# Forgetting attention's inverse roots: from ScalarE's Ln and Exp per four units to a Newton chain on GpSimd per two units

## The reference, cut to what matters

```python
q = x @ Wq; k = x @ Wk; v = x @ Wv
k = short_conv(k, kconv_w); v = short_conv(v, vconv_w)      # 4 taps, then silu
q = group_rmsnorm(q, qnw, H); k = group_rmsnorm(k, knw, H)  # x / sqrt(mean(x^2 per head) + 1e-6) * w
cum = jnp.cumsum(jax.nn.log_sigmoid(x @ Wf + bf), axis=1)
scores = q k^T / 8 + cum_t - cum_s, causal; attn = softmax(scores)
out = attn @ v
rms = jnp.sqrt(jnp.mean(jnp.square(out), axis=-1, keepdims=True) + EPS)
out = out / rms * onw * (g * jax.nn.sigmoid(g))             # g = x @ Wg
return out.reshape(Bx, Tx, H * Dh) @ Wo
```

## Time and profile before

| | |
|---|---|
| median of 3 runs | 2406.13 us (2402.49 to 2408.33) |
| profiled execution | 2402.83 us, of which 2401.0 us span |
| busy shares of the span | PE 80%, DVE 66%, ACT 59%, POOL 37% |
| the block that is changed | about 911 to 1960 us of the span |
| last unit begins its scores | 1914 us |

### The profile page before, as it was taken

The page is one execution under the profiler, slowest core; times in us unless marked ns, Lnnn a source line. Parts: engine busy times, 40 slices in busy tenths (PEclk is TensorE's granted clock), DMA queues, the critical chain, the costliest instruction groups (busy, mean ns, idle before and its releaser), DMA issues. The chain is left out here.

```text
span 2401.0 us, 35531 instructions
## 1 busy us (share of the span) xinstructions
PE 1915.7 (80%) x11731; PEld 871.1 (36%) x11731; DVE 1592.8 (66%) x2337; ACT 1406.1 (59%) x2262; POOL 890.3 (37%) x722
## 2 busy tenths in 40 slices
PE   4457886377775765799999999999999966599997
PEld 2113331343453422344444444444444422222222
DVE  4979995686347756678888888888887535511212
ACT  2446662333333434577777777777776533699994
POOL 0156663244014421345555455555555422500001
PEclk9769997598896987899999999999999988899998
DMA  2000000000000001111111111111112100412110
GB/s 90 0 14 0 0 0 0 1 1 1 0 1 0 1 7 47 47 49 58 57 57 58 57 58 57 57 58 58 57 58 64 45 23 11 121 40 54 47 47 36
DMA packets 66146, 86.15 MB, mean 36 GB/s; under 512 B 13344, under 2 KB 37216, under 8 KB 65888
## 3 DMA queue, kind: packets, MB, share of 16 engines
q1 hardware_dynamic: 60944, 81.37, 11.0%
q10 hardware_dynamic: 5040, 2.72, 0.4%
HBM read 72.12 MB, written 11.93 MB: 35 GB/s over the span
## 5 line engine op out<-in xcount | busy, mean ns | idle before, releaser
L1634 DVE SCALAR_TENSOR_TENSOR fu_kv<-fu_ps_kv,fa_vec,fu_kv 128x511 f32<-128x511 f32 x366 | 252.7, 738 | 7.1 <-ACT fu_kv L1542 6.3
L1991 ACT ACTIVATE rt_p<-rt_ps_s 128x1024 f32<-128x1024 f32 x256 | 240.4, 1042 | 26.2 <-PE rt_ps_o L1936 17.4
L1706 POOL TENSOR_TENSOR fu_p<-fu_p 128x768 f32<-128x768 f32 x64 | 116.7, 1824 | 262.2 <-PE fu_ps_n L1392 257.8
L1362 PE MATMUL fu_ps_s<-fu_qn,fu_kn 64*128 64x512 f32 (+3 forms) x1024 | 190.1, 469 | 7.5 <-ACT fu_p L1529 5.6
L601 POOL TENSOR_TENSOR scan_hC<-scan_h,scan_c 128x1024 f32<-128x1024 f32 x64 | 150.7, 2354 | 82.4 <-DVE scan_h L581 82.4
L1392 PE MATMUL fu_ps_n<-fu_p,fu_vt 128*64 128x512 f32 (+3 forms) x1024 | 166.3, 446 | 0.0
L526 PE MATMUL scan_ps_y<-scan_hC,w_ident 128*128 128x512 f32 x256 | 129.6, 630 | 41.5 <-POOL scan_hC L601 24.8
L581 DVE TENSOR_TENSOR_SCAN scan_h<-scan_dA,scan_ps_b 128x1024 f32<-128x1024 f32 x64 | 146.4, 2287 | 2.2
L1936 PE MATMUL rt_ps_o<-rt_p,rt_va 128*32 128x512 f32 x1024 | 138.1, 611 | 10.0 <-ACT rt_p L1991 8.1
L1717 POOL TENSOR_TENSOR fu_num<-fu_num,fu_sg 128x512 f32<-128x512 f32 x64 | 81.2, 1269 | 172.1 <-DVE fu_sg L1667 172.1
L1420 PE MATMUL fu_ps_kv<-w_XN,fa_wp 128*128 128x512 f32 x244 | 125.3, 637 | 17.6 <-DVE fu_cr L1599 15.3
(11 more groups left out here) (346 smaller groups left out, 4903.4 us busy)
## 6 DMA issues: line engine op xcount, KB each, us to landing
fu_rb<-rms_rows SPq DMA_DIRECT2D x256, 128.0 KB, 2.9
fu_ro<-rms_rows SPq DMA_DIRECT2D x128, 128.0 KB, 2.9
ra_stackq<-rope_parts SPq DMA_DIRECT2D x168, 32.0 KB
ra_stackk<-rope_parts SPq DMA_DIRECT2D x168, 32.0 KB
rms_rows<-fu_r SPq DMA_DIRECT2D x14, 192.0 KB, 2.1
w_X<-in_xT SPq DMA_DIRECT2D x4, 512.0 KB
fa_wp<-in_wp SPq DMA_DIRECT2D x8, 256.0 KB
fu_cr<-ncum_rows SPq DMA_DIRECT2D x128, 3.0 KB
```

The source lines that it names most:

```text
L1362: pe.matmul(sps[:, h, at:at + T - t * P], k[head(h), t * P:(t + 1) * P], q[head(h), t * P:T], start=(at == 0), stop=False)
L1634: dve.scalar_tensor_tensor(acc, projected(a, k)[:, 0:T - j], vec[:, a % GA, at:at + 1], acc, ALU.mult, ALU.add).then_inc(done, 1)
L1706: pool.tensor_tensor(tail, tail, P13[:, :, 0:3 * P], ALU.add).then_inc(s.d1, 1)
L1991: act.activation(pr[k % 2][i][:, :, :], sps[(U * n + u) % RING][:, :, :], ACT.Exp, scale=DH_B ** -0.5).then_inc(s.exp, 1)
```

## The change

WIN becomes 2, so a window slot is every second one (`i % 2 == 1`), and 32 windows take the place of 16. AHEAD stays 8 (now 4 WIN), OUT goes from 5 to 4 (WIN + 2), and with it the `wo` products move from odd to even slots.

ACT no longer does Ln, Exp and the preload. It gets the query and key sums instead (Identity with the epsilon as bias, `msq`), placed ahead of the four squares. DVE keeps the addition for outputs. SP folds the sums by SBUF-to-SBUF DMAs from MS ([rows, 512]) into VAR ([96, 64]), so that 32 partitions hold what were 4 rows. DVE makes a first guess of the inverse root from the bits (shift and xor, [96, 64]). POOL refines it: five operations in the window slot, six in the next, each waiting for the one before. SP stores the roots a slot later, and reads them for RB and RO from there on. On DVE, OG moves from the head of the slot to behind the taps, ahead of the bit operation and of reduce L1650. ACT's and DVE's special orders for window slots go.

```diff
-WIN = 4
+WIN = 2
+ROOT_SCALE = 1.8348544414191587e-20
-    AHEAD = 2 * WIN
-    OUT = WIN + 1
+    AHEAD = 4 * WIN
+    OUT = WIN + 2
+    ROWS = 2 * WIN
+    FOLD = 32 // ROWS
+    CUT = T // FOLD
-        q, o = i // WIN + 1, i // WIN - 1
+        q, o = i // WIN + 3, i // WIN - 1
+    def folded(j):
+        return 32 * (min(j, U // WIN) + max(j - 4, 0))
+        VAR, ROOT, STEP1, STEP2 = (st.sb(n, [96, CUT]) for n in ("var", "root", "step1", "step2"))
...
 # SP
-                    if i % WIN == 1 and windows(i - 1) != (None, None):
-                        j, r = (i - 1) // WIN + 1, rows_of(*windows(i - 1))
+                    if i % WIN == 1 and windows(i - 3) != (None, None):
+                        j, r = (i - 3) // WIN + 3, rows_of(*windows(i - 3))
                         sp.wait_ge(s.r, j + 1)
                         sp.wait_ge(s.put, 16 * j)
                         sp.dma_start(rows_dram[j, r, :], R[j % 2][r, :]).then_inc(s.put, 16)
-                    u = i - OUT
+                    u = i - OUT - 1
...
+                    if i % WIN == 1 and windows(i - 1) != (None, None):
+                        j, r = (i - 1) // WIN + 3, rows_of(*windows(i - 1))
+                        sp.wait_ge(s.r, j)
+                        sp.wait_ge(s.msq, min(j + 1, U // WIN))
+                        sp.wait_ge(s.mso, max(j - 3, 0))
+                        for g in range(3):
+                            if g < 2 and r.start == 0:
+                                sp.dma_start(VAR[32 * g:32 * g + 32, :], MS[32 * g:32 * g + ROWS, :]).then_inc(s.fold, 16)
+                            elif g == 2 and r.stop == 96:
+                                for h in range(2):
+                                    sp.dma_start(VAR[64 + 16 * h:80 + 16 * h, :], MS[64 + ROWS * h:64 + ROWS * h + WIN, :]).then_inc(s.fold, 16)
 # ACT
+                    if q is not None:
+                        act.wait_ge(s.sa, WIN * q + WIN)
+                        act.wait_ge(s.fold, folded(q))
+                        act.activation(MS[0:64, :], ssps[0:64, :], ACT.Identity, bias=w.eps_rms[0:64, 0:1]).then_inc(s.msq, 1)
...
-                        act.preload_act_table_set("natural_log_exp_and_others")
...
-                        act.activation(MS[r, :], MS[r, :], ACT.Ln).then_inc(s.ln, 1)
...
-                        act.activation(R[j % 2][r, :], MS[r, :], ACT.Exp, scale=-0.5).then_inc(s.r, 1)
 # DVE
-                    (OG at the head of the slot)
-                    if q is not None:
-                        dve.tensor_scalar(MS[0:64, :], ssps[0:64, :], RMS_EPS, None, ALU.add).then_inc(s.msq, 1)
+                    (behind the taps, ahead of reduce L1650)
+                    if real(o):
+                        dve.wait_ge(s.gated, o + 1)
+                        dve.wait_ge(s.ro, 32 * (o + 1))
+                        dve.wait_ge(s.wo, o // 2)
+                        dve.scalar_tensor_tensor(OG[o % 2][:, :], NUM[o % NR][:, :], ow[:, o % GA:o % GA + 1], RO[:, :], ALU.mult, ALU.mult).then_inc(s.og, 1)
+                    if q is not None or v is not None:
+                        j, r = (i - 1) // WIN + 3, slice(0, rows_of(q, v).stop)
+                        dve.wait_ge(s.fold, folded(j + 1))
+                        dve.wait_ge(s.r, j)
+                        dve.tensor_scalar(ROOT[r, :].bitcast(I32), VAR[r, :].bitcast(I32), 1, 0x7fffffff, ALU.logical_shift_right, ALU.bitwise_xor).then_inc(s.bits, 1)
 # POOL, behind its three additions; x, y, e, f = VAR, ROOT, STEP1, STEP2
+                    (window slot; each waits for the one before)
+                        pool.wait_ge(s.bits, j + 1)
+                        pool.tensor_scalar(y, y, ROOT_SCALE, None, ALU.mult).then_inc(s.ya, 1)
+                        pool.tensor_tensor(e, y, y, ALU.mult).then_inc(s.yb, 1)
+                        pool.tensor_tensor(e, e, x, ALU.mult).then_inc(s.yc, 1)
+                        pool.tensor_scalar(e, e, -0.5, 1.5, ALU.mult, ALU.add).then_inc(s.yd, 1)
+                        pool.tensor_tensor(y, y, e, ALU.mult).then_inc(s.y1, 1)
+                    (the slot behind it)
+                        pool.tensor_tensor(e, y, y, ALU.mult).then_inc(s.ye, 1)
+                        pool.tensor_tensor(e, e, x, ALU.mult).then_inc(s.yf, 1)
+                        pool.tensor_scalar(f, e, 0.375, -1.25, ALU.mult, ALU.add).then_inc(s.yg, 1)
+                        pool.tensor_tensor(f, f, e, ALU.mult).then_inc(s.yh, 1)
+                        pool.tensor_scalar(f, f, 1.875, None, ALU.add).then_inc(s.yi, 1)
+                        pool.wait_ge(s.put, 16 * max(j - 1, 0))
+                        pool.tensor_tensor(R[j % 2][r, :], y, f, ALU.mult).then_inc(s.r, 1)
```

More of the change, by code:

```diff
@@ L1288, in forget_units @@
         MS = st.sb("ms", [96, T])
-        R = [st.sb(f"r{k}", [96, T]) for k in range(2)]
+        VAR, ROOT, STEP1, STEP2 = (st.sb(n, [96, CUT]) for n in ("var", "root", "step1", "step2"))
+        R = [st.sb(f"r{k}", [96, CUT]) for k in range(2)]
         kvps, sps, mps = (st.ps(n, [P, 2, T]) for n in ("kv", "s", "m"))
         nps, ssps = st.ps("n", [P, T]), st.ps("ss", [P, T])
-        s = st.sems("set ones kvp tap t1 t2 cv th sk sv vt vc qp qc q2 k2 sa so dsq msq mso ln r rb ro put cr0 cr1 cr2 qn kn qm km "
+        s = st.sems("set ones kvp tap t1 t2 cv th sk sv vt vc qp qc q2 k2 sa so dsq msq mso fold bits ya yb yc yd y1 ye yf yg yh yi r rb ro put cr0 cr1 cr2 qn kn qm km "
                     "mx red hi ml rt rr sc ex pv d1 d2 ds n2 nc gp tg sg gated og wo x")
@@ L1322, in _ @@
                 sp.wait_ge(s.ones, 6)
-                for i in range(-AHEAD, U + OUT + 1):
+                for i in range(-AHEAD, U + OUT + 2):
                     u = i + 2
@@ L1342, in _ @@
                         sp.dma_start(rows_dram[j, r, :], R[j % 2][r, :]).then_inc(s.put, 16)
[L1343 removed]
+                    u = i - OUT - 1
                     if real(u):
[L1345 removed]
+                        sp.wait_ge(s.put, 16 * (u // WIN + 5))
                         sp.wait_ge(s.og, u)
                         for h in range(2):
[L1348 to L1349 removed]
+                            row = 2 * ROWS + WIN * h + u % WIN
+                            sp.dma_start(RO[head(h), :], roots_dram[u // WIN + 4, row:row + 1, :].broadcast_to([64, T])).then_inc(s.ro, 16)
+                    if i % WIN == 1 and windows(i - 1) != (None, None):
[9 more added lines that the diff above has]
+                                    sp.dma_start(VAR[64 + 16 * h:80 + 16 * h, :], MS[64 + ROWS * h:64 + ROWS * h + WIN, :]).then_inc(s.fold, 16)
                 for k in range(3):
@@ L1574, in _ @@
                         gates()
[L1575 to L1579, removed]
                     else:
@@ L2094, in constants @@
             sums[head == h, u, 2 * u + h] = 1.0 / DH_A
-            outs[head == h, u, 16 * h + u] = 0.25 / DH_A
-            c["seld"][:, h, u, 16 * h + u] = 1.0
+            outs[head == h, u, 2 * WIN * h + u] = 0.25 / DH_A
+            c["seld"][:, h, u, 2 * WIN * h + u] = 1.0
     c["selq"], c["selk"], c["selo"] = sums, (0.25 * sums).astype(np.float32), outs
```

50 lines of the change are left out of this document (27 added, 23 removed).

## The result

| | before | after |
|---|---|---|
| median of 4 runs each, one chip | 2407.23 us (2402.49 to 2408.98) | 2391.14 us (2389.57 to 2394.66) |
| ratio to before, 95% interval | | 0.9949 [0.9927, 0.9971] |
| profiled execution (span) | 2402.83 (2401.0) | 2391.51 (2389.5) |
| slots 4 to 55 | 781.0 | 787.6 |

The kernel became 16 us faster by these medians, with an interval of 7 to 18 us. The forecast was 2418 us, 15 more than the profiled execution before; the time lies in the range of 2387 to 2438, but on the other side of no change. One execution in this document, of the kernel before without its table loads, took 10182 us instead of some 2380 and is left out of its median.

What follows compares the result with a forecast made beforehand. PE was taken to bound the kernel. Steady stretch +28.9, slots 0 to 3 -4.3, ahead of them -1.5, drain -4 and tail -4 gave +15 us on 2402.8, so 2418 us, range 2387 to 2438.

Steps and rivals of the forecast that it cites:

- What bounds the kernel: Steady stretch of forgetting attention: PE sets the pace, busy 755.5 of 781.0 us, at most 25.5 us to win.
- Head of the window slot: Identity ahead of ACT's squares puts off DVE's addition and taps; PE waits 0.92 us for its last maxima, every window slot.
- OG in the window slot: OG, due at 10.42, waits for POOL's addition begun at 10.38; PE stalls 0.68 us at the transposes of V.
- both stalls: The forecast case: OG waits for POOL in window and even slots alike, 2418 us, own range 2409 to 2434, chance 0.52.
- rival C: Only one of OG's two stalls occurs: the pair of slots 30.5 us, the whole 2401 us; chance 0.15.
- OG in the even slot: OG waits for POOL's addition until 10.32, ends at 11.07; PE stalls 0.60 us at its wo products.
- the pair: One window slot of 15.22 us plus one even slot of 15.93: 31.15; 26 pairs 809.9 against 781.0, +28.9 us.
- Ahead of slot 0: One table load of 1.28 us and QN's wait for roots of 1.46 go, two Identities come: -1.5 us.
- Slots 0 to 3: First four slots, 56.0 us before: four of 12.7 plus one window's 0.92 make 51.7, so -4.3 us.
- Drain and tail: Drain: QN's wait for roots goes, -4 us; tail: last window holds back two units instead of four, about -4 us.
- The tables: ACT's table loads, 1.28 us each, are not the main price and lie mostly in ACT's spare time.
- Fold, chain, stores: Fold DMAs cost nothing with 1.8 us cover; POOL's chain of 2.0 and 2.4 us and later stores cost nothing on the path.

## Why the prediction was wrong, step by step

**What bounds the kernel** was read rightly: PE paces each slot, and all that the change does to the stretch is in two or three waits of PE.

**Head of the window slot: right.** Forecast: taps at 5.28, maxima at 8.59, stall 0.92. Measured: 5.25 (1417.38 - 1412.13), 8.56, and a slot of 14.51, which is 0.89 above 13.62. DVE's addition begins at 4.52 (1416.65 - 1412.13) where it was 3.98 and 4.56 was forecast: the Identity put it off by 0.54, where I had 0.58.

**OG in the window slot: wrong, and it decided the sign.** I had DVE at 10.42 and POOL's addition at 10.38. Measured are 10.39 and 10.40. The positions were right within 0.03 us, the order was not, and the stall of 0.68 was absent in 23 of 26 window slots. This is the step that failed; without its 17.7 us (26 times 0.68) the same sum would have come out at -3 instead of +15. The three others and the kernel with the bit operation first show the mechanism and its price, 0.37 and 0.33, so the size was also too large. That the order fell for OG was luck, as the 12 of 26 with the tables back show: the rows of before could not tell it. I had said that 0.04 us decides, and still gave both stalls a chance of 0.52. A margin that is smaller than the error of the terms that make it (the Identity alone I had put between 0.48 and 0.69) bears no more than an even chance; then the forecast would have been the case of one stall, 2401 by my own rival C, whose pair of 30.5 is the nearest to the measured 30.27.

**OG in the even slot: right, one size off.** The stall was 0.43 where I had 0.60 (the times as I wrote them give 0.58, and 0.65 for the window slot instead of 0.68). I let OG take its whole 0.75 once POOL was through; it ended 0.55 behind POOL's addition (1437.52 against 1436.97). The Trainium skill, page "SBUF — State Buffer", section "SBUF: two separate sides", says that the two exclude each other for whole instructions; the traces agree in who waits. That the one let in then still needs its whole time was my reading, and it was 0.2 us too much.

Together: the pair 31.15 forecast, 30.27 measured, 26 times 0.88 makes 22.9; the whole stretch came out 22.3 below the forecast, of the 26.5 us by which the profiled execution missed it.

**Ahead of slot 0: too small.** -1.5 forecast, -5.8 measured. Of it 0.8 lies ahead of the block. From the block's first operation on DVE to its first QN it is 53.53 before and 50.97 after, -2.6; the sum had -2.7 for the load and the wait for RB (which fell from 1.46 to 0.44) and +1.2 for the two Identities. From there to slot 0 it is 22.27 before at a granted clock of 0.62, and 19.83 after at 0.83, -2.4. Windows view from the first QN to slot 0 (busy and instructions of PE, PEld, DVE, ACT, POOL; clock; DMA), first of before, then of after:

```profile
965.07:987.34 22.27, 14.07 (x60) 5.70 (x59) 16.95 (x24) 8.69 (x15) 5.79 (x5) 0.62 0.15 48
```

```profile
961.70:981.53 19.83, 12.35 (x62) 4.84 (x63) 16.85 (x25) 9.41 (x16) 9.52 (x17) 0.83 0.20 55
```

Neither part is explained. With the loads back in, the kernel after takes 54.36 for the first of these, which speaks for the loads; but the kernel before without its loads still takes 53.24, and QN there waits 2.19 for RB. The second varies from 19.3 to 23.8 in the seven experiments on the kernel after, so why it fell, and what part of it is the clock, stays open too.

**Slots 0 to 3: near, with a slip.** I counted one window in them, but with windows every second slot there are two: slots 1 and 3 last 13.49 and 13.70, slots 0 and 2 12.45 and 12.76. With two the same sum gives 4 × 12.7 + 2 × 0.92 = 52.6 and -3.4, and -3.6 was measured. **Drain and tail: right.** -4 and -4 forecast, -3.8 and -3.6 measured. In the tail the roots' store came 6.4 later behind slot 63 (forecast 5.8), and from the store to the last addition it took 10.0 less (forecast 9.8). **Behind the block** -1.2 came that no step of the sum explains; work there is the same.

**The tables: wrong, though no term of the sum.** I wrote that they are not the main price and lie mostly in time that ACT has to spare. Two runs say otherwise: 17 to 24 us for their removal in the kernel before, 1.23 us for each window slot where they are put back. Of the old window slot with wo products the reading was right: 1.58 above PE's need, of which the loads are 0.49. But slot 5, the slot behind, slots 0 to 3 and the drain were not read for them, and they hold the larger part; and I took ACT's busy share for slack at every place where the loads would stand. In the sum it did little harm, because the sum was made from the slots of the new kernel and not from what is removed.

**Fold, chain, stores: right.** The fold's four transfers are issued from 1417.43 to 1420.30, and OG and the bit operation (0.18) don't wait for them in the slot shown. The steps of the chain take 0.24 to 0.37 each, with their waits 0.40, as estimated, and POOL has the time. What I left out is that their place matters as much as their length: where they end after SG, with gating queued behind them, they cost 1.36 us in each even slot (16.96 against 15.60). In the kernel after they end at 1425.90, ahead of SG at 1426.22.

## What to carry to other kernels

Where two engines share a port, do not only sum up durations: list for each slot which operation of the one starts within some tenths of a microsecond of one of the other, and give no order a chance above a half where the starts lie closer than your error. Then move the operation whose result is needed last behind the one that is needed first; that gained 11 us here, by moving OG and the bit operation behind the last reduce. Small operations queued on an engine with much spare time are free only if what stands behind them doesn't then run against an operation of the critical engine.

## What the runs showed of the hardware

- Two starts at most 0.02 us apart decided which engine waited, and the recorded times don't always show the order: among the 26 window slots of after there are ties at 0.00 of either outcome. In the kernel after DVE lost in 3 of 26, with the tables back, at the same places of the slot, in 12 of 26. The loser took 1.42 instead of 0.73 (POOL) or 1.27 instead of 0.74 (DVE).
- It was not only operations with two SBUF inputs that waited: the bit operation, [96, 64] int32 with one input, took 0.76 instead of 0.18 in three window slots of after, where POOL's addition came between OG and it.
- A DVE operation of 0.74 us that waited for POOL ended 0.54 to 0.56 us behind POOL's last operation, not 0.74: 1437.52 against 1436.97, 1427.11 against 1426.57, 1408.41 against 1407.85. In the last it waited through two of POOL's in a row. Where POOL's ended 0.07 behind its start it lost nothing.
- The block's first operation on DVE began between 904 and 915 us in these runs, though the work ahead of it was the same in all: starts of slots can be compared between kernels only from a point inside the block.
